# Band by GpSimd on the exponentials, and the NF4 planes summed by TensorE alone, in a fused four-layer kernel

## The chip, the cores and the metric

The kernel runs on one core of one Trainium2 chip. The metric is the device time of one launch in microseconds. Engines are named as in the profile: PE is TensorE (PEld its weight loads), DVE is VectorE, ACT is ScalarE, POOL is GpSimd, SP is SyncE, which only issues transfers.

## The reference

x has 16 batches of 128 rows by 512 columns. Four layers are added to it in turn, each on its layer norm: a first attention, a feed-forward layer with NF4 weights, a cross attention, and a layer of 32 experts. Only two pieces matter here. The first attention sees a batch as 512 tokens of 128 channels (8 heads of 16), and a query attends only to keys at a distance of 64 or less:

```python
scores = jnp.einsum('bqhd,bkhd->bhqk', q, k) / jnp.sqrt(jnp.asarray(d, q.dtype))
band = jnp.abs(idx[:, None] - idx[None, :]) <= local_size        # local_size = 64
scores = jnp.where(band[None, None], scores, neg)
attn = jax.nn.softmax(scores, axis=-1)
o = jnp.einsum('bhqk,bkhd->bqhd', attn, v).reshape(n, t, e)
```

The weights of the feed-forward layer go through NF4 and back: blocks of 64 are divided by their largest magnitude, each value is replaced by the nearest of 16 levels, and the result is multiplied by the (again quantized) block scale.

```python
idx = jnp.argmin(jnp.abs(scaled[:, None] - NF4), axis=-1)
```

## The kernel before

Everything that the change touches is in `phase_layer0_attention`, the first 490 us. Each engine has a program of its own, written out by hand, and they meet only by semaphores; the order on an engine is the order of the code. All of them run `batches`, a body for each of the 16 batches i (the first two and the last two written out, the rest as a hardware loop over pairs). In a batch there are two units u = 2i and 2i + 1, one for each half of the heads, and in a unit eight steps c.

For the attention, a step c has three parts on TensorE: the maxima of the *next* batch (`smax`, L505: two products of 192 or 256 columns in one of two banks `ps_max`), the scores of this one (`scores`), and now and then a piece of other work. In `scores` one bank `ps_sc` (again two, taken in turn) holds one head against two key tiles, transposed: keys on the partitions, the window of 256 queries around each key tile in the columns. The first product into the bank (L520) is identity times `band_mask`, 448 columns, which puts 0 inside the band and -1e30 outside; the two products of L525 add the scores to it. ScalarE turns the bank into exponentials in `probs_t` (`exps`, L383, 448 columns f32). When four steps are done, `pv` (L537) multiplies the probabilities with the values: at c = 5 for the first half of a unit's steps, at c = 1 of the next unit for the second half. VectorE takes the band's row maxima from `ps_max` (`take_max`, L776, which adds the same mask), two instructions a step. A score may start when the exponential two steps before it is done, a maximum when the one two before it is taken.

Between these runs the NF4 round trip of the weights, one chunk of 512 columns a unit, 33 chunks m in all. VectorE scales a chunk (L898), compares it with eight steps (`nf4_compare`, L908: result (value > step) times the level's height, as f16, two comparisons in each of c = 0 to 3), and at c = 4 adds the eight planes pairwise to four (L912, 128x2048 elements). ScalarE makes seven more planes with a sign function (L377). TensorE sums the four and the seven planes in `ps_nf4` during the next unit (`nf4_sum`, L571), as the table `NF_AT` has it for c = 0 to 7, and VectorE multiplies the sum with the block scale (L918). So VectorE's and ScalarE's work in a unit belongs to chunk m and TensorE's to chunk m - 1.

GpSimd builds constants at the start (the mask with `affine_select`, L294 and L297), and issues the transfers of the block scales through DRAM: L308 and L311 (`gather_maxima`), L315 and L319 (`spread_scales`). After about 117 us it is idle to the end of the stage.

## Time and profile before

| | us |
|---|---|
| median of 3 runs | 1466.27 |
| lowest, highest | 1461.33, 1466.6 |
| profiled execution, first to last instruction | 1463.7 |
| median of the runs less that span | 2.6 |

Busy in the whole span: TensorE 93%, VectorE 69%, ScalarE 54%, GpSimd 17%. These shares are means over four very different stages. The change touches the first, so only what stands in 0 to 490 us says what it is worth. An engine's busy time there is that of drawn instructions; matmuls are drawn with a tail that overlaps the next, so pitches, from start to start, tell more of TensorE. The granted TensorE clock was 0.98 of full speed between 100 and 200 us and 1.00 from there to 400, that is 2.4 GHz.

### The profile page before, as it was taken

Reading aid. Unit: us, or ns where it says so; the run is one execution under the profiler, and the core shown is the slowest. Engines: PE = TensorE matmul, PEld = TensorE weight load, DVE = VectorE, ACT = ScalarE, POOL = GpSimd, SP = SyncE. Lnnn points to the kernel's source line nnn. Section 1 sums busy time; section 2 is a strip of 40 time slices with the busy share of each in tenths; the row PEclk is TensorE's granted clock in tenths of the full one; section 3 lists DMA queues with packets and bytes.
Section 4 is the critical chain, followed back from the end, with each engine's and each line's share of the span. In section 5 each row is a group of like instructions: output and inputs, shape, how many; then the busy total and the mean of one; then the engine's idle time right before and its main releaser. Section 6 shows DMA issues by size and latency. Waiting matters only on the chain. (4 is left out here: it accounts for less than half of the span.)

```text
span 1463.7 us, 28639 instructions
## 1 busy us (share of the span) xinstructions
PE 1354.5 (93%) x8666; PEld 813.1 (56%) x8666; DVE 1002.8 (69%) x3234; ACT 791.5 (54%) x1802; POOL 249.2 (17%) x265
## 2 busy tenths in 40 slices
PE   3678999999999799999989999999789999999998
PEld 1345555555555444444455555555434777777774
DVE  8889999999997646456546788887659654545211
ACT  4777888888888733332357677776530233332331
POOL 4100000000000100000010000002411255555552
PEclk7699999999999999999999999999999999999999
DMA  8534344343440300000020000000322588888885
GB/s 261 145 87 99 91 107 106 86 119 90 107 104 17 145 1 0 0 0 0 0 75 15 16 16 14 14 1 2 146 85 93 184 247 251 255 257 246 255 233 115
DMA packets 63186, 149.52 MB, mean 102 GB/s; under 512 B 10792, under 2 KB 27830, under 8 KB 58892
## 3 DMA queue, kind: packets, MB, share of 16 engines
q1 hardware_dynamic: 49836, 115.70, 26.1%
q0 software_dynamic: 13280, 32.93, 9.6%
q8 instruction: 38, 0.62, 0.2%
q14 instruction: 32, 0.26, 0.1%
HBM read 113.21 MB, written 35.39 MB: 102 GB/s over the span
## 5 line engine op out<-in xcount | busy, mean ns | idle before, releaser
L776 DVE CUSTOM_DVE_ANT_0 masked_scores<-ps_max,band_mask 128x192 bf16<-128x192 f32 (+1 forms) x512 | 177.2, 383 | 20.5 <-PE ps_max L505 13.9
L383 ACT ACTIVATE probs_t<-ps_sc 128x448 f32<-128x448 f32 x256 | 138.7, 542 | 80.4 <-PE ps_sc L525 78.1
L1255 PE MATMUL f_ps<-f_xt,w_t 128*128 (+1 forms) x704 | 160.2, 382 | 2.5 <-ACT w_t L1310 2.5
L377 ACT ACTIVATE nf_above<-nf_scaled,nf_sign_at 128x512 f16<-128x512 bf16 x231 | 161.5, 715 | 0.0
L2803 DVE TENSOR_TENSOR d_inter<-d_silu_g,d_su 128x384 f32<-128x384 f32 x32 | 17.7, 554 | 159.6 <-PE d_su L2487 154.4
L1927 ACT ACTIVATE c_probs<-d_sg,c_negmax 128x128 f32<-128x128 f32 x256 | 90.3, 365 | 58.1 <-DVE c_negmax L2012 57.7
L1255 PEld LDWEIGHTS f_ps<-f_xt,w_t 128*128 128x128 bf16 x704 | 69.3, 98 | 86.7 <-issue 5.0
L2320 POOL DMA_INDIRECT out<-d_h,d_scatter_now x64 | 97.2, 1519 | 108.3 <-DMA out<-d_h,d_scatter_now 92.9
L505 PE MATMUL ps_max<-k_stack,q_stack 96*128 96x192 bf16 (+1 forms) x512 | 96.5, 272 | 19.8 <-DVE row_max L776 13.8
L2671 DVE TENSOR_SCALAR d_onehot<-d_slot_no,d_pos 128x192 bf16<-128x192 bf16 x512 | 101.0, 288 | 0.3 <-PE d_lb L2388 0.3
L505 PEld LDWEIGHTS ps_max<-k_stack,q_stack 96*128 96x128 bf16 x512 | 46.2, 101 | 92.1 <-issue 46.9
L520 PE MATMUL ps_sc<-band_mask,identb 128*128 128x448 bf16 x256 | 92.7, 362 | 2.5 <-ACT probs_t L383 2.5
L2481 PE MATMUL d_su<-d_h,d_wgu 128*128 128x192 f32 x512 | 93.7, 337 | 1.4 <-DVE d_h L2790 1.0
L525 PE MATMUL ps_sc<-q_stack,k_stack 98*128 98x192 bf16 (+1 forms) x512 | 93.2, 263 | 0.0
L2481 PEld LDWEIGHTS d_su<-d_h,d_wgu 128*128 128x128 f32 x512 | 84.4, 194 | 9.8 <-issue 9.8
L2487 PE MATMUL d_su<-d_h,d_wgu 128*128 128x192 f32 x512 | 88.4, 326 | 0.0
L1429 DVE SCALAR_TENSOR_TENSOR f_h<-f_ps,f_h_scale,f_silu 128x512 f32<-128x512 f32 x44 | 32.9, 748 | 76.7 <-PE f_ps L1255 76.6
L2487 PEld LDWEIGHTS d_su<-d_h,d_wgu 128*128 128x128 f32 x512 | 84.1, 190 | 0.0
L2012 DVE TENSOR_REDUCE c_negmax<-d_sg 128x4 f32<-128x512 f32 x64 | 44.0, 688 | 50.7 <-PE d_sg L1705 49.9
L571 PE MATMUL ps_nf<-nf_above,nf_half_step 128*128 128x512 f16 x231 | 75.8, 380 | 0.0
L1336 ACT ACTIVATE f_hparts<-f_h 128x512 f16<-128x512 f32 x44 | 27.7, 630 | 86.0 <-DVE f_h L1429 86.0
L525 PEld LDWEIGHTS ps_sc<-q_stack,k_stack 98*128 98x128 bf16 x512 | 51.3, 100 | 28.7 <-issue 3.0
(381 smaller groups left out, 2830.1 us busy)
## 6 DMA issues: line engine op xcount, KB each, us to landing
d_wgu<-in_ex_gu SPq DMA_DIRECT2D x32, 1024.0 KB
d_wdown<-in_ex_d SPq DMA_DIRECT2D x32, 512.0 KB
dr_parts<-qk_parts SPq DMA_DIRECT2D x32, 384.0 KB, 4.8
q_stack<-dr_parts SPq DMA_DIRECT2D x32, 192.0 KB, 2.7
k_stack<-dr_parts SPq DMA_DIRECT2D x32, 192.0 KB, 3.3
out<-x_sb SPq DMA_DIRECT2D x21, 256.0 KB, 2.2
nf_w<-in_nf_w POOLq DMA_DIRECT2D x3, 1408.0 KB, 10.2
q_stack<-dr_parts SPq DMA_DIRECT2D x32, 128.0 KB, 2.4
```

The lines of the kernel that those rows point to most:

```text
L377: act.activation(above[:, g, k, :], lvl[:, g, :], ACT.Sign, bias=cut[:, k - NDV:k - NDV + 1]).then_inc(s_sg, 1)
L383: act.activation(pt[:, c, :], SP[c % 2][:].rearrange("p a w -> p (a w)")[:, a:z], ACT.Exp, scale=D0 ** -0.5).then_inc(s_e, 1)
L505: mm = pe.matmul(m[:, k, off:off + hi - lo], qst[0:96, b, h, qt * P:qt * P + P], kst[0:96, b, h, lo:hi], start=True, stop=True)
L520: pe.matmul(s[:].rearrange("p a w -> p (a w)")[:, a:z], identb[:], mask[:].rearrange("p a w -> p (a w)")[:, a:z], start=True, stop=False)
L525: mm = pe.matmul(s[:, k, off:off + hi - lo], kst[0:98, b, h, kt * P:(kt + 1) * P], qst[0:98, b, h, lo:hi], start=False, stop=(k == 1))
L776: op = dve.tensor_tensor_reduce(masked[:, c % 2, k, off:off + hi - lo], M[c % 2][:, k, off:off + hi - lo], mask[:, k, off:off + hi - lo], ...
L1255: mm = pe.matmul(bank[:], w12[:, m, kt, ft * P:(ft + 1) * P], xt[:, q, kt, bass.ds(g * N, N)], start=(kt == 0 and q == 0), stop=(kt == KT ...
L1927: op = act.activation(pr[:, ot % 2, j, :], SB[ot % 2][:, j, :], ACT.Exp, bias=nm[:, ot % 2, j:j + 1], accum_out=sm[:, bb, 4 * ot + j:4 * o ...
L2320: pool.indirect_dma_start(out, bass.IndirectOffsetOnAxis(ap=sst[rows_of[a], par, a:a + 1], axis=0), yo[a][:, par, :], None, compute_op=ALU ...
L2481: mm = pe.matmul(GP[:, it, :], wg[:, par, t, it * P:(it + 1) * P], xt[:, par, t, :], start=(t == 0), stop=(t == KT - 1))
L2487: mm = pe.matmul(UP[:, it, :], wg[:, par, t, FI + it * P:FI + (it + 1) * P], xt[:, par, t, :], start=(t == 0), stop=(t == KT - 1))
L2671: op = dve.tensor_scalar(oh[:, half, tl, jj, :], ios[:], pos[:, half * HT + tl, bass.ds(4 * q + jj, 1)], None, ALU.is_equal)
```

## The change

It has two parts.

1. *The band.* The mask product L520 goes; the scores' two products each start their own region of the bank. ScalarE's exponential is then of unmasked scores, and GpSimd sets the elements outside the band to zero afterwards, by two `affine_select` a step, each over 2 x 128 columns of `probs_t`, in place (`band`). `pv` waits for the select's semaphore `s_in` and no longer for the exponential's. `probs_t` gets full windows (8 x 2 x 256), whose outer 64 columns are set to zero once and aren't written by the exponentials. GpSimd's transfers of the block scales now stand between its selects. The maxima still use the mask on VectorE.
2. *The planes.* The add L912 goes; TensorE sums all eight comparison planes and the seven sign planes, 15 matmuls a chunk in place of 11.

```diff
@@ gpsimd @@
+            def band(u, c):
+                pool.wait_ge(s_e, 8 * u + c + 1)
+                pool.nop(nofuse=True)
+                low, high = pt[:, c, :, 0:P], pt[:, c, :, P:WIN]
+                pool.affine_select(out=low, in_=low, compare_op=ALU.is_ge, fill=0.0, base=0,
+                                   pattern=[[0, 2], [1, P]], channel_multiplier=-1)
+                pool.affine_select(out=high, in_=high, compare_op=ALU.is_ge, fill=0.0, base=0,
+                                   pattern=[[0, 2], [-1, P]], channel_multiplier=1).then_inc(s_in, 1)
+            def body(j, i, b, first, last, final):
+                for c in range(8):
+                    band(2 * i, c)
+                if first:
+                    pool.wait_ge(s_sc, 1)
+                    spread_scales(0, 1)
+                for c in range(8):
+                    band(2 * i + 1, c)
+                    if c == 4 and isinstance(i, int) and i == 1:
+                        pool.wait_ge(s_sc, 2)
+                        spread_scales(1, 3)
+                if first:
+                    pool.wait_ge(s_am, 5)
+                    gather_maxima(1, 3)
@@ scores @@
-                pe.matmul(s[:].rearrange("p a w -> p (a w)")[:, a:z], identb[:],
-                          mask[:].rearrange("p a w -> p (a w)")[:, a:z], start=True, stop=False)
...
-                                   qst[0:98, b, h, lo:hi], start=False, stop=(k == 1))
+                                   qst[0:98, b, h, lo:hi], start=True, stop=True)
@@ pv @@
-                pe.wait_ge(s_e, 8 * u + 4 * kp + 4)
+                pe.wait_ge(s_in, 8 * u + 4 * kp + 4)
@@ NF4 @@
-            NF_AT = [[], [0, 2], [4, 6], [8], [9, 10], [11], [12, 13], [14]]
+            NF_AT = [[], [0, 1], [2, 3], [4, 5], [6, 7, 8], [9, 10], [11, 12], [13, 14]]
...
-                if c == 4:
-                    dve.wait_ge(s_ab, NF_INC * m + 4)
-                    dve.tensor_tensor(above[:, g, 0:8:2, :], above[:, g, 0:8:2, :], above[:, g, 1:8:2, :], ALU.add).then_inc(s_ab, 1)
```

How this moves instructions is seen at two places. The first is TensorE in the loop, steps c = 1 and 2 of a unit, before:

```order
L520 MATMUL ps_sc<-band_mask,identb 128x448 [waits a_exp]
L525 MATMUL ps_sc<-q_stack,k_stack 128x192
L525 MATMUL ps_sc<-q_stack,k_stack 128x256
L530 ISA
L537 MATMUL ps_o<-probs_t,v_ones 32x256 [waits a_exp]
L537 MATMUL ps_o<-probs_t,v_ones 32x256 x3
L537 MATMUL ps_o<-probs_t,v_ones 32x192 x4
L565 ISA
L571 MATMUL ps_nf<-nf_above,ident_f 128x512 [waits a_nf4_done,a_nf4_above]
L571 MATMUL ps_nf<-nf_above,ident_f 128x512
```

and now, for the same steps of an earlier unit (the line numbers are those of the changed kernel):

```order
L549 MATMUL ps_sc<-q_stack,k_stack 128x192 [waits a_exp]
L549 MATMUL ps_sc<-q_stack,k_stack 128x256
L561 MATMUL ps_o<-probs_t,v_ones 32x256 [waits a_probs_in_band]
L561 MATMUL ps_o<-probs_t,v_ones 32x256 x3
L561 MATMUL ps_o<-probs_t,v_ones 32x192 x4
L595 MATMUL ps_nf<-nf_above,ident_f 128x512 [waits a_nf4_done,a_nf4_above]
L595 MATMUL ps_nf<-nf_above,ident_f 128x512
```

The mask product is gone and the probability product waits for another semaphore; at c = 4 three planes are summed where there were two, and the order of everything else is kept. The second place is GpSimd around its first transfer of block scales (`dr_rep<-sc_bf`), before:

```order
L303 DMA nf_w<-in_nf_w 128x4x1408
L315 DMA dr_rep<-sc_bf 88x128 [waits a_sc]
L319 DMA block_scale<-dr_rep 128x11x8 [waits a_rep_wr]
L308 DMA dr_sc<-absmax 128x11x8 [waits a_block_max]
L308 DMA dr_sc<-absmax 128x4x22
```

and now:

```order
L344 AFFINE_SELECT probs_t<-probs_t 128x2x128 [waits a_exp]
L346 AFFINE_SELECT probs_t<-probs_t 128x2x128
L316 DMA dr_rep<-sc_bf 88x128 [waits a_sc]
L320 DMA block_scale<-dr_rep 128x11x8 [waits a_rep_wr]
L344 AFFINE_SELECT probs_t<-probs_t 128x2x128 [waits a_exp]
L346 AFFINE_SELECT probs_t<-probs_t 128x2x128
```

Eight pairs of selects now stand ahead of the transfer, and the ninth waits behind it and behind what it waits for.

## Rows read from the trace of the kernel before

**Rows 1.** The windows view, two stretches; "(x...)" counts instructions.

```profile
core 0: us, PE busy (x) PEld busy (x) DVE busy (x) ACT busy (x) POOL busy (x), PEclk, DMA share, GB/s
459.00:478.00 19.00, 18.45 (x151) 9.84 (x149) 11.35 (x30) 17.81 (x35) 0.00 (x0) 1.00 0.05 16
200.00:226.14 26.14, 24.96 (x197) 14.59 (x197) 24.80 (x100) 21.61 (x40) 0.00 (x0) 1.00 0.41 101
```

**Rows 2.** Line L810 (add to x): its register step, once a batch.

```profile
L810 DVEq FUSED_REGOPS  x12: 65/65/65, 144.8 to 432.3; - x12
```

**Rows 3.** Waits, 200 to 400 us: total, times, longest us.

```profile
PEld ps_max L505 <- DVE row_max L776: 5.3, 19, 0.4
...
DVE masked_scores L776 <- PE ps_max L505: 4.1, 8, 0.7
```

**Rows 4.** Groups, 200 to 400 us: busy us, mean ns, idle before.

```profile
L571 PE MATMUL ps_nf<-nf_above,nf_half_step 128*128 128x512 f16 x106 | 35.3, 379 | 0.0
L908 DVE TENSOR_SCALAR nf_above<-nf_scaled 128x512 f16<-128x512 bf16 x124 | 29.9, 281 | 0.0
...
L912 DVE TENSOR_TENSOR nf_above<-nf_above 128x2048 f16<-128x2048 f16 x15 | 18.2, 1210 | 0.0
```

**Rows 5.** Timeline, TensorE at 306 and 480: start us, duration us, instructions.

```profile
305.94 0.35 PE L520 MATMUL ps_sc<-band_mask,identb 128*128 128x448 bf16 x1
...
306.13 0.25 PE L525 MATMUL ps_sc<-q_stack,k_stack 98*128 98x192 bf16 x1
...
480.25 1.03 PE L571 MATMUL ps_nf<-nf_above,ident_f 128*128 128x512 f16 x4
```

**Rows 6.** Timeline, GpSimd's selects at the start.

```profile
1.87 0.28 POOL L292 TENSOR_SCALAR_AFFINE_SELECT ident<-ident 128x128 f32<-128x128 f32 x1 [0.24 <-POOL band_mask L289]
2.12 0.28 POOL L292 TENSOR_SCALAR_AFFINE_SELECT identb<-identb 128x128 bf16<-128x128 bf16 x1
2.37 0.61 POOL L294 TENSOR_SCALAR_AFFINE_SELECT band_mask<-band_mask 128x512 bf16<-128x512 bf16 x1
```

**Rows 7.** Timeline, 8.5 to 17 us: GpSimd's memset and VectorE's conversions.

```profile
8.61 6.92 POOL L327 MEMSET k_stack<- 2x8192 bf16 x1
...
10.37 5.24 DVE L818 CAST ident_f<-ident 128x128 f16<-128x128 f32 x1
...
15.75 0.21 DVE L820 TENSOR_SCALAR nf_half_step<-ident 128x128 f16<-128x128 f32 x1
```

**Rows 8.** Views of L2671 (1183.5 to 1187.6 us) and L2057: min/median/max ns.

```profile
L2671 DVE TENSOR_SCALAR d_onehot<-d_slot_no,d_pos x16: 249/257/570, 1183.7 to 1187.2; 128x192 bf16<-128x192 bf16 x16
...
L2057 DVE TENSOR_TENSOR x_sb<-x_sb,c_out x16: 677/680/692, 812.9 to 1052.7; 128x512 f32<-128x512 f32 x8, 128x512 f32 x8
```

**Rows 9.** Timeline, GpSimd in three later stretches.

```profile
1015.23 17.08 POOL L1608 TENSOR_SCALAR c_next_rows<-x_sb,c_next_mv,c_next_rstd 128x512 f32<-128x512 f32 x8 [24.03 <-DVE c_next_rstd L2113]
...
1106.52 0.50 POOL L2283 COPY d_quad_vals<-d_slot_vals 128x384 bf16<-128x384 bf16 x1 [23.38 <-DVE d_tmp L2761]
...
1183.92 1.09 POOL L2283 COPY d_quad_vals<-d_slot_vals 128x384 bf16 x1
```

**Rows 10.** Timeline, 314 to 318 us: exponential and probability product.

```profile
314.77 0.54 ACT L383 ACTIVATE probs_t<-ps_sc 128x448 f32<-128x448 f32 x1 [0.45 <-PE ps_sc L525]
...
316.98 0.96 PE L537 MATMUL ps_o<-probs_t,v_ones 128*32 128x256 f32 x16
```

**Rows 11.** Timeline, 478 to 486 us: the stage's end.

```profile
478.01 0.59 PEld L537 LDWEIGHTS ps_o<-probs_t,v_ones 128*32 128x32 f32 x16 [0.76 <-ACT probs_t L383]
...
482.81 1.23 DVE L912 TENSOR_TENSOR nf_above<-nf_above 128x2048 f16<-128x2048 f16 x1
...
485.22 1.02 PE L571 MATMUL ps_nf<-nf_above,ident_f 128*128 128x512 f16 x4 [0.18 <-ACT nf_above L377]
```

**Rows 12.** Timeline, GpSimd's transfers of the block scales.

```profile
90.69 0.79 POOL L311 DMA_DIRECT2D sc_blocks<-dr_sc  x1 [4.34 <-DMA dr_sc<-absmax]
...
114.97 1.91 POOL L319 DMA_DIRECT2D block_scale<-dr_rep  x2 [1.65 <-DMA dr_rep<-sc_bf]
```

More of the change, by code:

```diff
@@ L109, in phase_layer0_attention @@
     mparts = sb("max_parts", [16, 2, P], BF16)
-    pt = sb("probs_t", [P, 8, 2 * WIN - BAND], F32)
+    pt = sb("probs_t", [P, 8, 2, WIN], F32)
     oc = sb("o_cols", [P, D], F32)
@@ L174, in phase_layer0_attention @@
     s_s, s_e, s_pv = sem("a_scores"), sem("a_exp"), sem("a_pv")
+    s_in, s_pad = sem("a_probs_in_band"), sem("a_probs_pad")
     s_oc, s_oT, s_rs, s_on = sem("a_o_copy"), sem("a_o_turn"), sem("a_o_recip"), sem("a_o_norm")
@@ L204, in phase_layer0_attention @@
     PRODUCTS = [(qst, 0, [(0, 0, 2), (2, 0, 3), (5, 0, 1)]), (kst, 1, [(0, 0, 3), (3, 0, 1), (4, 0, 2)])]
-    NF_INC = 5
+    NF_INC = 4
     MEAN_AT = D - 4
@@ L336, in _ @@
             load_nf(2)
-            pool.wait_ge(s_sc, 1)
-            spread_scales(0, 1)
-            pool.wait_ge(s_am, 5)
-            gather_maxima(1, 3)
-            pool.wait_ge(s_sc, 2)
-            spread_scales(1, 3)
+            def band(u, c):
[20 more added lines that the diff above has]
+                    gather_maxima(1, 3)
+            pool.wait_ge(s_ko, 1)
+            pool.memset(pt[:, 0:4, 0, 0:BAND], 0.0).then_inc(s_pad, 1)
+            pool.wait_ge(s_pad, 1)
+            pool.memset(pt[:, 4:8, 1, WIN - BAND:WIN], 0.0).then_inc(s_pad, 1)
+            pool.wait_ge(s_pad, 2)
+            batches(pool, body)
         @block.scalar
@@ L382, in exps @@
                 a, z = kept(c // 4)
-                act.activation(pt[:, c, :], SP[c % 2][:].rearrange("p a w -> p (a w)")[:, a:z], ACT.Exp, scale=D0 ** -0.5).then_inc(s_e, 1)
+                act.activation(pt[:, c].rearrange("p a w -> p (a w)")[:, a:z], SP[c % 2][:].rearrange("p a w -> p (a w)")[:, a:z], ACT.Exp, scale=D0 ** -0.5).then_inc(s_e, 1)
             def o_copy(u, g):
@@ L518, in scores @@
                 s = SP[c % 2]
-                a, z = kept(kp)
-                pe.matmul(s[:].rearrange("p a w -> p (a w)")[:, a:z], identb[:],
-                          mask[:].rearrange("p a w -> p (a w)")[:, a:z], start=True, stop=False)
                 for k in range(2):
@@ L537, in pv @@
                         mm = pe.matmul(O[32 * j:32 * j + 32, lo:hi], va[:, b, kt, 4 * g + j, :],
-                                       pt[:, 4 * kp + j, k * WIN + off - kept(kp)[0]:k * WIN + off - kept(kp)[0] + hi - lo],
+                                       pt[:, 4 * kp + j, k, off:off + hi - lo],
                                        start=(kt == 0), stop=(kt == QT - 1), skip_group_check=True)
@@ L573, in nf4_sum @@
                     mm.then_inc(s_lm, 1)
-            NF_KS = [0, 2, 4, 6] + list(range(8, NLV))
-            NF_AT = [[], [0, 2], [4, 6], [8], [9, 10], [11], [12, 13], [14]]
+            NF_KS = list(range(NLV))
+            NF_AT = [[], [0, 1], [2, 3], [4, 5], [6, 7, 8], [9, 10], [11, 12], [13, 14]]
             def nf4_mean(lo, hi):
```

## The prediction, made before the changed kernel was run

> **What bounds the kernel now.** I read the windows first, since the change touches one stage only, the first attention (0 to 490 us of the span); then the groups of instructions in its steady part, the waits there, and last the timeline, where pitches and gaps can be seen. One batch takes (432.3 - 144.8) / 11 = 26.14 us: the line that adds to x runs once a batch, and its register step ran twelve times between those two starts [rows 2]. In a stretch of exactly one batch VectorE is busy 24.80 us, TensorE 24.96 us (with modelled ends), ScalarE 21.61 us and GpSimd 0 [rows 1]. The reader is to see three engines near full and one empty. Which of the first two is the bound is decided by the waits: VectorE waited on TensorE for only 4.1 us in 200 us, and TensorE's loads on VectorE's maxima for 5.3 us, on the same two banks [rows 3]. The stretch 459 to 478, the last batch, settles it. There are no maxima of a next batch there, VectorE is busy 11.35 of 19.00 us, and the same 16 exponentials take 19 us in place of 26 [rows 1]. That batch also lacks 32 maximum products and the projections on TensorE, so it doesn't prove VectorE alone, but it is then ScalarE that is full (17.81 of 19.00). I take VectorE as the bound of the steady batch, with TensorE close behind: TensorE's matmuls are shown with a tail (a 448-column product is drawn at 0.35 us, but the next starts 0.19 us later), so its true load is less than it looks [rows 5].
>
> **Part one: the sum of the planes.** It removes one VectorE add of 128x2048 f16 per chunk, 33 in all, 1.21 us each [rows 4]: two per batch, 2.42 us of VectorE's 24.80. It adds four matmuls of 512 columns per chunk on TensorE. Four such matmuls in a row take 1.03 us [rows 5], and one alone is drawn at 0.38 [rows 4]: (1.03 - 0.38) / 3 = 0.217 us each, so 8 x 0.217 = 1.7 us per batch. They are laid out two or three behind each score; the order shows none on its own wait.
>
> **Part two: the band.** It removes the mask product of each score from TensorE, 16 a batch at a pitch of 0.19 us [rows 5], 3.0 us. TensorE so ends 3.0 - 1.7 = 1.3 us a batch lighter, and stays behind VectorE. ScalarE's work is unchanged. GpSimd gets two selects of 128x256 f32 behind each exponential, 32 a batch. The trace has selects of 128 columns (start to start 0.25 us, drawn at 0.28) and of 512 (0.61) [rows 6]: (0.61 - 0.28) / 384 = 0.86 ns a column, so 256 columns have a pitch near 0.36 us, and 32 of them are 11.5 us of a batch. GpSimd is thus at work some 45% of the time, and keeps up.
>
> **The wait for the band.** The probability products now wait for the select instead of the exponential. From the end of an exponential to both selects is about 0.1 + 0.36 + 0.39 = 0.85 us. The last exponential that a second-half product needs ended at 314.77 + 0.54 = 315.31, and the product began at 316.98: 1.7 us of slack [rows 10]. The first-half product stands behind the score two places after its last exponential, as this one does, and is no nearer. So the selects hide, as long as they aren't held up by more than 0.8 us. Behind a product that waited stand all of TensorE's later maxima and scores. I count 0 in the steady batches.
>
> **What GpSimd costs VectorE.** This is the term that decides, and it isn't in the diff. At the start a VectorE cast of 128 columns is drawn at 5.24 us, and it ends just when GpSimd's 6.92 us memset does; the same size takes 0.21 us once GpSimd is idle [rows 7]. Later, GpSimd's copy of 384 columns (L2283) takes 0.50 us at 1106.5, and 1.09 us at 1183.9 beside VectorE's tensor_scalars on bf16 (L2671); in that stretch one of the tensor_scalars takes 570 in place of 249 ns [rows 8, 9]. So a VectorE operation of this kind and a GpSimd operation exclude each other, and one meeting costs VectorE about 570 - 249 = 0.32 us. The 16 comparisons a batch (L908, 281 ns, in pairs) are of that kind [rows 4]. Not all VectorE work is: the add of two SBUF tensors at L2057 took 677 to 692 ns in all 16 places, which come about every 16 us, so that one at least fell into the 17 us in which GpSimd ran without a gap [rows 8, 9]; and reads of PSUM, the maxima above all, weren't seen held. Bounds per batch: below, 0 meetings, 0 us; above, every comparison meets a select, 16 x 0.32 = 5.1 us. I take 5 meetings: GpSimd works 45% of the time, so about 4 of 8 pairs find a select under way, and now and then one slips in between the two of a pair. 5 x 0.32 = 1.6 us.
>
> A rule of the Trainium skill speaks against this change more strongly (SBUF — State Buffer, Who interferes with whom): GpSimd has only the port pair that VectorE uses as its second, and "a DVE instruction with two SBUF inputs contends with a GpSimd instruction that reads SBUF". By that the three kinds with two SBUF inputs would be held too, which is the third rival below; without the rule the sum stays as it is. The trace agrees on the exclusion for the comparisons' kind and shows no such delay at L2057.
>
> **The sum**, against the profiled execution: span 1463.7 us, with 2.6 us around it up to the median of 1466.27.
> - Batches 0 to 14: 15 x (-2.42 + 1.6) = -12.3 us.
> - Last batch: 0. ScalarE is the bound there, and its work is the same [rows 1].
> - The tail (478 to 490): here TensorE is followed in order. Eight more matmuls at 0.217 are +1.7; the last probability product had waited for its exponential, so the selects' 0.9 us is fully seen. The add at 482.81 to 484.04 was over before the sum that needed it began at 485.22, so its removal gives nothing [rows 11]. +2.6 us.
> - The start: GpSimd's DMAs of the block scales now stand between selects. Its wait of 4.34 us for a DMA (before L311) holds the selects of the third group, whose product comes 8 scores later; three more issues and a wait near 1.7 us stand inside the fourth group [rows 12]. I take +1.0, between 0 and about 6.
> - Sum: -8.7 us. 1466.3 - 8.7 = 1457.6 us.
>
> **What is late next.** Without the add VectorE has 22.4 us, with the meetings 24.0; TensorE some 23.7 as drawn; ScalarE 21.6. All three lie within 10%, so each loses something to the others' order; the 1.34 us that VectorE now idles per batch is kept as it is.
>
> **The rivals.**
> - *Hardly a meeting.* GpSimd's selects fall mostly beside the maxima. One or no meeting a batch: 15 x (-2.42 + 0.3) + 3.6 = -28; with none -32.7. 1434 to 1438 us. For it: selects follow exponentials, comparisons follow maxima, and their phases may stay apart. Against: the rows of the gather stage, where meetings came in each group.
> - *Slower: the selects and comparisons meet nearly every time.* The place is VectorE at L908; the price 0.32 us a meeting; it decides from 2.42 / 0.32 = 7.6 meetings a batch on. When VectorE is delayed, it frees TensorE's bank later, scores come later and bunch, and the selects bunch with them. With 11 of 16: 15 x (3.5 - 2.42) + 3.6 = +20: 1486 us; with all 16, +44: 1510.
> - *Two-input operations are held as well.* Third parts (2), scaled weights (2) and the gate (1) are five more a batch, at half chance and 0.32: 0.8 us. 15 x (-2.42 + 1.6 + 0.8) + 3.6: about 1470 us.
> - *The wait for the band takes the removed work's place.* If GpSimd is held by comparison pairs (0.48 us) and one slow operation, the 0.8 us of spare at the second-half product is used up. Four products a batch at 0.5 us are 2.0, against the 1.3 that TensorE gains: 15 x 0.7 + 3.6, about 1480 us if TensorE is then the bound. Against it: the 1.7 us of slack [rows 10].
>
> **How the numbers follow.** The smallest change a measurement of this kernel can tell is about 0.5%, 7.3 us: faster is below 1459, slower above 1473.6. The forecast case (3 to 7 meetings, 1448 to 1467) has 0.40, of which 0.24 falls below 1459 and 0.16 within. Hardly a meeting: 0.24, faster. Two-input: 0.12, of it 0.08 within and 0.04 slower. Band wait: 0.08, 0.02 within and 0.06 slower. Meetings nearly always: 0.16, slower. Together: faster 0.48, the same 0.26, slower 0.26. The range reaches from no meeting (1434) to 11 or 12 of 16 (1488); the forecast case's own is 1448 to 1467.
>
> **What would show it.** The group of the 128x2048 add is gone and VectorE's share in a batch falls below 24 us. The comparisons' median stays near 281 ns, but their maximum rises to 600 ns or so, and their mean to 281 + 1600 / 16, near 380 ns; at 281 the first rival holds, over 430 the second. Third parts (L751), scaled weights (L898) and the gate (L757) keep the lengths that they have before, or the third rival holds. Selects are drawn near 0.39 us, some at 0.6 to 0.9. In the waits, the probability products show GpSimd as releaser only in the last batch and the tail. The register step of the add to x comes every 25.3 us. The forecast is wrong if that period lies above 26.1, or if TensorE or ScalarE shows idle time ended by GpSimd in the steady batches.

## The result, and the profile after

The changed kernel takes 1469.54 us (median of 20 runs, 1467.01 to 1473.52), the kernel before 1466.02 us (20 runs): a ratio of 1.0031, interval 1.0021 to 1.0040. By the prediction's bound of 0.5% this is no change. It is slower all the same, by 3.5 us in the medians and by 3 to 6 us by the interval, where 8.7 us less were forecast. Its profiled execution took 1467.35 us, with a span of 1465.6 us.

In the changed file the lines have moved: L908 is now L932 (comparisons), L898 L922, L751 L775, L757 L781, L776 L800 (maxima), L571 L595 (planes), L537 L561 (probability product), L810 L834 (add to x), L383 L410 (exponential). The selects are L344 and L346.

The windows, of one batch and of a stretch inside the last one, answer to [rows 1]; line L834's register step to [rows 2].

```profile
core 0: us, PE busy (x) PEld busy (x) DVE busy (x) ACT busy (x) POOL busy (x), PEclk, DMA share, GB/s
200.00:225.76 25.76, 23.68 (x190) 13.81 (x189) 23.63 (x102) 21.87 (x40) 15.19 (x33) 1.00 0.40 103
456.00:475.00 19.00, 17.02 (x141) 9.19 (x141) 9.65 (x28) 17.41 (x34) 12.13 (x31) 1.00 0.06 17
```

```profile
L834 DVEq FUSED_REGOPS  x12: 65/65/65, 143.2 to 426.6; - x12
```

The period is (426.6 - 143.2) / 11 = 25.76 us, 0.38 less than before. VectorE and TensorE both lost over 1 us of work a batch, and both now stand idle for some 2 us. The waits from 200 to 400 us (total, times, longest) say on whom:

```profile
POOL probs_t L344 <- ACT probs_t L410: 83.7, 102, 1.9
...
DVE masked_scores L800 <- PE ps_max L532: 13.2, 22, 1.0
PEld ps_max L532 <- DVE row_max L800: 11.7, 35, 0.5
...
PE ps_g L538 <- DVE o_rows L827: 6.7, 8, 0.8
PE ps_g L538 <- DVE x_sb L834: 5.2, 7, 0.8
```

In [rows 3] the first two waits between VectorE and TensorE were 4.1 and 5.3 us; the last two, TensorE's transposes of the maxima waiting at the turn of a unit, had these rows in the kernel before:

```profile
PE ps_g L511 <- DVE o_rows L803: 5.1, 8, 0.6
...
PE ps_g L511 <- DVE x_sb L810: 3.9, 7, 0.6
```

So each engine waits longer for the other than before. The probability product waits for GpSimd in no row of this stretch. The groups there (busy us, mean ns, idle before), and the views of four lines of VectorE (min/median/max ns), answer to [rows 4, 8]:

```profile
L344 POOL TENSOR_SCALAR_AFFINE_SELECT probs_t<-probs_t 128x256 f32<-128x256 f32 x125 | 64.6, 517 | 83.7 <-ACT probs_t L410 83.7
L346 POOL TENSOR_SCALAR_AFFINE_SELECT probs_t<-probs_t 128x256 f32<-128x256 f32 x125 | 60.4, 483 | 0.0
L932 DVE TENSOR_SCALAR nf_above<-nf_scaled 128x512 f16<-128x512 bf16 x124 | 35.1, 323 | 0.0
L922 DVE SCALAR_TENSOR_TENSOR nf_scaled<-nf_w,absmax_recip 128x512 bf16 x16 | 12.5, 779 | 0.0
```

```profile
L932 DVE TENSOR_SCALAR nf_above<-nf_scaled x264: 270/286/865, 45.0 to 480.2; 128x512 f16<-128x512 bf16 x132
L922 DVE SCALAR_TENSOR_TENSOR nf_scaled<-nf_w,absmax_recip x33: 672/693/975, 43.5 to 466.8; 128x512 bf16 x24, 128x512 bf16<-128x512 bf16 x9
L775 DVE TENSOR_TENSOR qk_parts<-qk_resid,qk_parts x32: 683/692/877, 18.0 to 414.1; 128x512 bf16<-128x512 f32 x32
L781 DVE TENSOR_TENSOR gated<-relu_o,ctx_tile x16: 686/686/847, 112.4 to 484.4; 128x512 f32<-128x512 f32 x16
```

Meetings are there and are cheap: the comparisons' mean is 323 ns against 281 before, 16 x 0.042 = 0.67 us a batch, and the two scaled weights cost 2 x (0.779 - 0.678) = 0.20 more. The timeline of VectorE shows the single meetings. These are the held comparisons and the two scaled weights of one batch; a comparison that isn't held takes about 0.28 us (0.47 to 0.49 a pair), a scaled weight 0.67:

```profile
225.85 0.50 DVE L932 TENSOR_SCALAR nf_above<-nf_scaled 128x512 f16<-128x512 bf16 x1
226.27 0.89 DVE L922 SCALAR_TENSOR_TENSOR nf_scaled<-nf_w,absmax_recip 128x512 bf16 x1
228.29 0.69 DVE L932 TENSOR_SCALAR nf_above<-nf_scaled 128x512 f16<-128x512 bf16 x2
...
239.50 0.67 DVE L922 SCALAR_TENSOR_TENSOR nf_scaled<-nf_w,absmax_recip 128x512 bf16 x1
240.66 0.70 DVE L932 TENSOR_SCALAR nf_above<-nf_scaled 128x512 f16<-128x512 bf16 x2
```

The pairs left out (at 236.19, 237.28 and 239.10, and from 248.21 to the end of the batch at 251.6) aren't held. So three comparisons and one scaled weight are held a batch, each by some 0.21 us. GpSimd pays most of it: an undisturbed select is drawn at 0.41 us, the mean is 0.50, and 32 x 0.09 = 2.9 us a batch.

Just behind the rolled loop (the hardware loop over batches 2 to 13) is something the forecast did not have. The timeline of TensorE (start, duration, instructions, idle before):

```profile
427.57 0.27 PE L538 MATMUL ps_g<-ident,row_max 128*16 128x128 f32 x1 [0.66 <-issue]
427.68 0.38 PE L532 MATMUL ps_max<-k_stack,q_stack 96*128 96x256 bf16 x2
427.89 0.35 PE L549 MATMUL ps_sc<-q_stack,k_stack 98*128 98x192 bf16 x2
428.18 0.95 PE L561 MATMUL ps_o<-probs_t,v_ones 128*32 128x256 f32 x12
431.68 0.52 PE L561 MATMUL ps_o<-probs_t,v_ones 128*32 128x192 f32 x4 [2.55 <-issue]
```

TensorE stands 2.55 us between the twelfth and the thirteenth of the sixteen drawn matmuls of one probability product (the profile draws each of its eight twice). It waits for no engine ("issue"); TensorE has no such gap there in the kernel before. The tail's timeline answers to [rows 11]:

```profile
475.72 0.96 PE L561 MATMUL ps_o<-probs_t,v_ones 128*32 128x256 f32 x16 [0.70 <-POOL probs_t L346]
...
483.79 1.89 PE L595 MATMUL ps_nf<-nf_above,ident_f 128*128 128x512 f16 x8 [0.18 <-ACT nf_above L404]
485.51 1.67 PE L595 MATMUL ps_nf<-nf_above,nf_half_step 128*128 128x512 f16 x7
```

Here the product does wait for the select, and eight matmuls stand where four stood.

### The profile page after: what moved, and what is told of

It reads as the page before. It is cut to its first block and busy times, and to the rows that moved or that the text cites. A ratio compares the mean times of both kernels' runs of the same rounds, so it can differ in the third digit from the quotient of the medians.

```text
span 1465.6 us, 29315 instructions
## 1 busy us (share of the span) xinstructions
PE 1336.3 (91%) x8542; PEld 800.7 (55%) x8542; DVE 980.7 (67%) x3201; ACT 794.8 (54%) x1802; POOL 488.0 (33%) x779
## 5 line engine op out<-in xcount | busy, mean ns | idle before, releaser
L800 DVE CUSTOM_DVE_ANT_0 masked_scores<-ps_max,band_mask 128x192 bf16<-128x192 f32 (+1 forms) x512 | 176.6, 384 | 32.8 <-PE ps_max L532 29.6
L344 POOL TENSOR_SCALAR_AFFINE_SELECT probs_t<-probs_t 128x256 f32<-128x256 f32 x256 | 128.2, 501 | 173.7 <-ACT probs_t L410 173.4
L410 ACT ACTIVATE probs_t<-ps_sc 128x448 f32<-128x448 f32 x256 | 139.1, 544 | 71.3 <-PE ps_sc L549 65.8
L346 POOL TENSOR_SCALAR_AFFINE_SELECT probs_t<-probs_t 128x256 f32<-128x256 f32 x256 | 123.6, 483 | 2.0 <-ACT probs_t L410 2.0
L1623 POOL TENSOR_TENSOR x_sb<-x_sb,c_bp 128x512 f32 x16 | 21.1, 1319 | 210.1 <-DVE c_xq L1995 210.0
L1615 POOL MEMSET c_k_diag<- 128x4096 f32 x1 | 3.5, 3512 | 248.0 <-DVE c_xq L1995 248.0
L595 PE MATMUL ps_nf<-nf_above,ident_f 128*128 128x512 f16 x264 | 79.9, 388 | 2.9 <-DVE nf_w L939 2.7
```

The source lines that it names most:

```text
L344: pool.affine_select(out=low, in_=low, compare_op=ALU.is_ge, fill=0.0, base=0, pattern=[[0, 2], [1, P]], channel_multiplier=-1)
L346: pool.affine_select(out=high, in_=high, compare_op=ALU.is_ge, fill=0.0, base=0, pattern=[[0, 2], [-1, P]], channel_multiplier=1).then_inc ...
L410: act.activation(pt[:, c].rearrange("p a w -> p (a w)")[:, a:z], SP[c % 2][:].rearrange("p a w -> p (a w)")[:, a:z], ACT.Exp, scale=D0 ** ...
L800: op = dve.tensor_tensor_reduce(masked[:, c % 2, k, off:off + hi - lo], M[c % 2][:, k, off:off + hi - lo], mask[:, k, off:off + hi - lo], ...
```

## The experiments

The table gives every run by its ratio to the kernel before of the same job and by five numbers of its one profile: the period of the rolled batches (register steps over 11), the first batch behind the loop, the time from the last add to x but one to the last (the tail, with the last batch's end), TensorE's own stall behind the loop, and for how long in that batch the granted clock was 0.50, that is 1.2 GHz.

| run | median us | ratio (interval) | period | behind the loop | tail | stall | low clock |
|---|---|---|---|---|---|---|---|
| before | 1466.02 | | 26.14 | 26.57 | 10.53 | none | 3.4 |
| changed | 1469.54 | 1.0031 (1.0021-1.0040) | 25.76 | 28.91 | 13.03 | 2.55 | 3.4 |
| e1_planes_only | 1477.26 | 1.0088 (1.0071-1.0104) | 26.85 | 25.73 | 12.26 | none | none |
| e2_band_only | 1479.17 | 1.0105 (1.0086-1.0124) | 26.75 | 26.16 | 11.63 | none | 3.4 |
| e3_no_band | 1462.34 | 0.9990 (0.9978-1.0002) | 25.34 | 28.17 | 12.28 | 2.26 | 3.4 |
| e4_spare_tile | 1469.11 | 1.0028 (1.0014-1.0042) | 25.75 | 28.91 | 12.30 | 2.54 | 3.4 |
| e5_no_add | 1459.41 | 0.9966 (0.9953-0.9979) | 25.82 | 24.36 | 10.53 | none | none |
| e6_no_mask | 1460.65 | 0.9983 (0.9970-0.9996) | 25.57 | 25.32 | 11.19 | none | 3.4 |
| e7_add_at_end | 1468.26 | 1.0029 (1.0017-1.0041) | 25.75 | 29.20 | 11.29 | 2.85 | 3.4 |
| e8_changed_again | 1469.10 | 1.0034 (1.0021-1.0047) | 25.75 | 29.47 | 13.01 | 3.13 | 3.4 |
| e9_turn_later | 1468.36 | 1.0023 (1.0008-1.0037) | 25.51 | 30.43 | 13.03 | 3.27 | 6.8 |
| e10_before_turn_later | 1458.46 | 0.9951 (0.9935-0.9967) | 25.67 | 24.83 | 10.53 | none | none |
| e11_32_nops | 1469.76 | 1.0043 (1.0027-1.0059) | 25.75 | 30.54 | 13.03 | 2.82 | 6.8 |
| e12_before_both_turns | 1456.11 | 0.9951 (0.9934-0.9968) | 25.45 | 24.58 | 10.53 | none | none |
| e13_changed_both_turns | 1462.25 | 0.9985 (0.9972-0.9998) | 25.27 | 25.45 | 13.11 | 1.58 | none |
| e14_16_nops | 1470.66 | 1.0044 (1.0029-1.0060) | 25.75 | 28.68 | 13.02 | 2.32 | 3.4 |
| e15_8_nops | 1469.24 | 1.0030 (1.0017-1.0043) | 25.75 | 29.21 | 13.02 | 2.86 | 3.4 |
| e16_nops_inside | 1469.12 | 1.0028 (1.0010-1.0046) | 25.76 | 30.17 | 13.02 | 2.97 | 6.8 |
| e17_nops_behind | 1470.86 (one) | | 25.76 | 30.37 | 13.01 | 2.40 | 6.8 |
| e18_four_halved | 1466.03 | 1.0014 (1.0003-1.0025) | 25.76 | 24.39 | 13.03 | none | none |

### Each part alone

e1 is the kernel before with the planes summed unfolded and the mask product kept:

```
-    NF_INC = 5
+    NF_INC = 4
-    NF_KS = [0, 2, 4, 6] + list(range(8, NLV))
+    NF_KS = list(range(NLV))
     (NF_AT as in the changed kernel)
-    if c == 4: dve.wait_ge(...); dve.tensor_tensor(above[:, g, 0:8:2, :], ..., ALU.add)
```

> The kernel before with the second part of the change alone: VectorE's pairwise add of planes is gone, TensorE sums 15 planes a chunk, the mask product stays and GpSimd has no selects. Theory A (VectorE stays the bound of a steady batch, and GpSimd's selects take the gain away): period 26.14 - 2.42 + something under 0.5, about 24.0 to 24.3 us in place of 26.14, the whole 25 to 32 us faster than before. Theory B (TensorE becomes the bound as soon as VectorE is lighter, whoever does the band): TensorE gains 1.7 us of work a batch, the period stays at 25.8 us or above, the whole within 6 us of before.

e2 is the changed kernel with the add kept and 11 plane products, the reverse of those lines.

> The kernel before with the first part of the change alone: no mask product, the band set to zero by GpSimd behind each exponential, VectorE's add of planes kept. Theory A (selects cost VectorE, which is the bound): VectorE gets about 0.9 us more a batch and saves nothing, so the period is 26.6 to 27.2 us and the whole 8 to 20 us slower than before. Theory B (TensorE the bound): TensorE is 3.0 us a batch lighter, so the whole is faster by up to 10 us.

Each part alone makes the kernel slower, by 0.9 and 1.05%. For e2 that is what the first theory had; e1 came out slower than either of its theories. One batch of e1 in the windows view (columns as above), then one of e2:

```profile
200.00:226.85 26.85, 25.98 (x204) 15.57 (x204) 22.90 (x99) 21.55 (x40) 0.00 (x0) 1.00 0.38 98
```

```profile
200.00:226.75 26.75, 22.36 (x184) 12.83 (x180) 25.80 (x102) 21.59 (x40) 14.60 (x33) 1.00 0.39 98
```

In e1 the full engine is TensorE: it has 1.7 us more, and the period is 0.71 us longer although VectorE lost 2.42. In e2 it is VectorE, 25.80 of 26.75 us, and the meetings lengthen what is full. So the parts can't be added up: each part takes from one engine and gives to the other, and the two together undo each other's harm.

### The selects: port or wait?

e3 has no selects (the band isn't applied), e4 runs them on a spare tile, and the product waits for the exponential alone:

```
 e3  -  band(2 * i, c) ... batches(pool, body)
     -  pe.wait_ge(s_in, 8 * u + 4 * kp + 4)
     +  pe.wait_ge(s_e, 8 * u + 4 * kp + 4)
 e4  +  ge(pool, s_in, 8 * u + c)             # each pair of selects behind the one before
     -  low, high = pt[:, c, :, 0:P], pt[:, c, :, P:WIN]
     +  low, high = spare[:, :, 0:P], spare[:, :, P:WIN]
     and the same wait as e3
```

> The changed kernel with the band left out: neither mask product nor selects, probability products wait for the exponentials; GpSimd issues its transfers as before the change. Theory A (selects are what eats the gain): period near 23.8 to 24.2 us against 25.76 in the changed kernel, the whole 25 to 35 us faster than before. Theory B (the selects are cheap, the rest of the chain between TensorE, ScalarE and VectorE is the limit): period 25 us or more, the whole under 15 us faster. Theory C (the later stages are slower whatever the first stage does): the stages behind 490 us take some 2 to 3 us longer than in the kernel before here too.

> The changed kernel, but GpSimd's selects, in number, shape and time of release the same, work on a spare tile, and the probability products wait for the exponentials; the band is left out of the result. Only what GpSimd does to VectorE is left, not the wait for it. If the meetings on VectorE are the cost, it is as the changed kernel in the steady batches: 25.6 to 25.8 us a batch. If the wait for the band is the cost, it is as the one without selects, near 24 us. In the last two batches and the tail the wait for the selects is gone in any case, 2 to 4 us of the 5 us that the changed kernel loses there.

With the selects and no wait on them the period is 25.75 us, as changed; without the selects it is 25.34. So the wait for the band costs nothing in a steady batch, and GpSimd's work beside VectorE costs 0.41 us. VectorE's busy time in one batch grows by more, 0.69 us (23.63 against 22.94 in e3), or 0.87 by the means of the two groups above. e3's group of comparisons is back at 281 ns:

```profile
L912 DVE TENSOR_SCALAR nf_above<-nf_scaled 128x512 f16<-128x512 bf16 x124 | 29.9, 281 | 0.0
```

In the tail the wait is seen: 13.03 against 12.28 and 12.30 us. With the last batch, 0.6 us shorter in e4, that is 1.3 us, where the expectation of e4 had 2 to 4.

### One relief at a time

e5 is the kernel before without the add (TensorE still sums 11 planes, so the four odd planes of each chunk aren't in the sum), e6 without the mask product (no band on the scores):

```
 e5  -  dve.tensor_tensor(above[:, g, 0:8:2, :], ..., ALU.add)
 e6  -  pe.matmul(s[...][:, a:z], identb[:], mask[...][:, a:z], start=True, stop=False)
```

> The kernel before with VectorE's pairwise add taken out and nothing put in its place: TensorE still sums 11 planes a chunk, so four comparison planes are left out of the weights. VectorE is 2.42 us a batch lighter, TensorE is unchanged. Theory V (the prediction's: VectorE bounds the steady batch): period 26.14 - 2.42 and a little, 23.8 to 24.5 us, the whole 25 to 35 us faster. Theory T (TensorE and its waits at the turn of a unit bound it): period 25.8 to 26.1 us, the whole faster by 0 to 5 us.

> The kernel before with the mask product taken out and nothing put in its place: the band is left out of the result. TensorE is 3.0 us a batch lighter, VectorE, ScalarE and GpSimd are unchanged. Theory V (VectorE is the bound): period 26.0 us or more, the whole within 3 us of before. Theory T (TensorE is the bound, half of what it is relieved of comes through until VectorE is full): period 24.9 to 25.8 us, the whole 6 to 18 us faster.

2.42 us less for VectorE bring 0.32 us a batch, 3.0 us less for TensorE 0.57, both together (e3, with 1.7 us given back to TensorE) 0.80. The waits of e5, 200 to 400 us:

```profile
DVE masked_scores L776 <- PE ps_max L505: 16.0, 24, 1.0
...
PEld ps_max L505 <- DVE row_max L776: 11.9, 35, 0.4
```

VectorE waited 4.1 us for the maxima's products before [rows 3] and now 16.0: of the 2.42 us removed, (16.0 - 4.1) / 7.7 batches = 1.5 us come back as waiting. TensorE's loads, too, wait more for VectorE (11.9 us against 5.3), though VectorE has less to do. Neither engine as a whole is the bound, then. What else could be, the points at which the two hand over to each other, is tested under "The turns". The period of e6 is as expected by its second theory, but the whole fell by less than the 6 us it had as its least.

### The tail, and the changed kernel again

e7 is the changed kernel with the add and 11 products kept for the last two chunks, e8 the changed kernel unedited.

```
+  if c == 4 and isinstance(m, int) and m >= NCH - 2:
+      dve.tensor_tensor(above[:, g, 0:8:2, :], ..., ALU.add).then_inc(s_ab, 1)
```

> The changed kernel with VectorE's pairwise add kept for the last two chunks only, where the steady batches are over and VectorE idles; TensorE then sums 11 planes for these two and 15 for the others. If the eight further matmuls stand on the path at the stage's end, as the prediction's tail term has it, the stretch from the second last to the last add to x is 1.6 to 1.8 us shorter than in the changed kernel (13.0 us there), and the whole 1.5 to 2 us faster than it, that is 0 to 3 us slower than before. If that stretch hangs on something else, it stays at 13 us.

> The changed kernel once more, for a second profile and more times on the chip that the others share. Ratio to before 1.002 to 1.004. If the stages behind 490 us, which took 977.5 us in its first profile against 975.1 us in that of the kernel before, are longer for a reason in the kernel, they take 977 us or more again; if that was the spread between executions, the second profile lies anywhere between 974 and 979.

The tail gives back 1.7 us, the eight matmuls as priced. The whole hardly shows it (1.0029 against 1.0034): the stall and the start differ as much from one execution to the next.

### The turns

TensorE's transposes of a unit's maxima (max_t) stand in front of the next unit's scores and wait there for VectorE. e10 moves the one of the second half one step later in the kernel before, and VectorE's step that reads it behind that step's comparisons; e9 does so in the changed one. e12 and e13 also put a probability product ahead of each such transpose.

```
 e9, e10    -  if c == 0: (wait) max_t(2 * i + 1, 1)
            +  if c == 1: (wait) max_t(2 * i + 1, 1)
               and max_parts(2 * i + 1, 1) on VectorE behind the comparisons of step 1,
               no longer ahead of them
 e12, e13   +  pv(2 * i - 1, 1 - b, 1, 1) before that wait
            +  pv(2 * i, b, 0, 1) before the waits of max_t(2 * i + 2, 0)
```

> The changed kernel with one handshake moved: at the turn to a new batch TensorE turns the row maxima (the transposition at L538 into ps_g) one step later, behind the scores of step 1 and no longer behind those of step 0, and VectorE reads them behind its comparisons of step 1. All work is the same. In the changed kernel TensorE stands 1.7 us a batch before these transpositions, waiting for VectorE's last work of the unit before (o_rows, the add to x). Theory T (the batch is bound by the two engines waiting for each other in order, at the turn of a unit, and not by either one's work): moving one of the two takes 0.3 to 0.8 us out of a batch, period 25.0 to 25.5 us, the whole 5 to 12 us faster than the changed kernel. Theory W (work bounds it): period 25.7 us as before.

> The kernel before with the same handshake moved by one step. TensorE stands 1.5 us a batch before the transpositions there. Theory T: period 25.6 to 25.9 us in place of 26.14, the whole 3 to 9 us faster than before. Theory W: 26.1 us.

> The kernel before with the transposes that VectorE waits for issued one step later, as in the run before, and now both handshakes of a batch behind a probability product: TensorE has that product to do while VectorE ends what it needs. Theory A (what bounds the batch is that two nearly full engines meet at the turn of each unit): VectorE's waits for TensorE and TensorE's for VectorE shrink, period 25.0 to 25.5 us against 25.67, whole 1452 to 1457 us. Theory B (the work of either engine bounds it and the meeting is only where it shows): period 25.6 to 25.8, whole 1457 to 1460. If VectorE in its turn gets its operand too late, the period is above 26 and the whole above 1462.

> The changed kernel with the same two moves as the run beside it. Theory A (the meeting of the engines bounds the batch): the relief of VectorE comes through, period 25.0 to 25.4 us against 25.76 as changed and 25.51 with one move, whole 1460 to 1466 us. Theory B (TensorE's own work, 22.2 us and more of each batch, bounds it by now): period 25.5 to 25.8, whole 1467 to 1470. By both the stall after the loop's end and the longer tail (13 us after the last batch but one) stay.

No engine does less work, and the period of the kernel before falls by 0.47 us with one move and 0.69 with both, more than the whole change under study brings (0.38). Of the two waits at the turn, 5.1 and 3.9 us, the second is gone from the waits of e10 and both from those of e12. That of the changed kernel falls by 0.25 and 0.49. The whole of e9 gained far less than the 5 to 12 us expected; its batch behind the loop is the second longest of the table. In e12 VectorE has hardly a gap left, one batch of it:

```profile
200.00:225.45 25.45, 24.83 (x198) 14.51 (x197) 24.89 (x102) 21.38 (x39) 0.00 (x0) 1.00 0.41 104
```

VectorE's idle time is 0.56 us there, where it was 1.34 [rows 1]. In e13 a new wait appears, the product that now comes earlier waits for the selects:

```profile
PEld ps_o L561 <- POOL probs_t L346: 7.2, 8, 0.9
```

e10 and e12 beat both kernels (0.9951 each); between these two the time can't be told apart, though the period can.

### The stall behind the loop

e11, e14, e15 put 32, 16 and 8 empty instructions on TensorE ahead of the loop, e17 16 behind it, e16 one ahead of each score.

```
+  for k in range(32):            # 16 in e14, 8 in e15
+      pe.nop(nofuse=True)
   batches(pe, body)
```

> The changed kernel with 32 empty TensorE instructions ahead of the rolled loop, which do no work and only move where TensorE's later instructions lie in its code. Theory A (the 2.3 to 3.3 us in which TensorE stands in the middle of a probability product just after the loop hang on where its code lies): the stall leaves that place or shrinks, the time between the last batch's predecessor and it (28.9 and 29.5 us in two profiles of the changed kernel) falls to 25.5 to 27, and the whole to 1465.5 to 1467.5 us, 0.999 to 1.001 of the kernel before. Theory B (it does not hang on the place): the stall stays at 2.3 to 3.3 us, the batch at 28.5 to 29.5, the whole at 1468 to 1470 (1.0015 to 1.0035). The period of the rolled batches is 25.75 us by both.

> The changed kernel with 16 empty TensorE instructions ahead of the rolled loop, half as many as the run with 32, which left the 2.3 to 3.3 us stall of TensorE at the same instruction (after the twelfth matmul of the first probability product behind the loop). Theory A (32 was a whole number of the pieces in which code arrives, so that run moved nothing): here the stall moves to another instruction or goes, and with it some 2 us of the batch after the loop (28.9 to 30.3 us in the changed kernel; 26 to 27 without it) and of the whole, 1466 to 1468 us. Theory B (the place of the code doesn't matter): the stall stays after the twelfth matmul, 2.3 to 3.3 us, the whole 1468.5 to 1470.5.

> The changed kernel with 8 empty TensorE instructions ahead of the rolled loop. Theory A: the stall moves to an instruction between those of the run with none and the run with 16, or goes. Theory B: it stays after the twelfth matmul of that product, 2.3 to 3.3 us, the whole 1468.5 to 1470.5 us.

> The changed kernel with one empty TensorE instruction ahead of each score, 16 a batch, 32 in the rolled loop's body of two batches. By my count of two instructions a matmul (weights and product) the kernel before has 32 x (1 mask product) less 16 x (1 plane sum) more in it than the changed one, 32 a body, so that the loop now ends as far from its start as there. Theory C (the stall behind the loop hangs on how long the loop's body is, as profiles of bodies 32 longer, 32 shorter and 48 longer show none): it is gone, the batch behind the loop takes 26 to 27.5 us, the whole 1466 to 1468.5 us if the empty instructions cost the steady batch nothing (period 25.75). Theory D (it does not, but on what the changed kernel's TensorE does): the stall stays at 2.3 to 3.3 us and the whole at 1468.5 to 1471.

> The changed kernel with 16 empty TensorE instructions just behind the rolled loop, run once. Theory C (a fixed number of instructions from the loop's start): the stall comes some 8 matmuls earlier in the work, after about the fourth of the product's sixteen matmuls, and is as long or longer. Theory D: it stays after the twelfth.

The stall stayed at the same matmul in e11, e14, e15 and e17. This is no evidence: the built program keeps one of the empty instructions ahead of the loop and none of the 16 behind it, so these four are in effect the changed kernel again (and give its spread: stall 2.32 to 3.13 us in its six profiles, batch behind the loop 28.7 to 30.5). e16 keeps four in the loop's body of two batches, not the 32 it was meant to add, so it doesn't test its theories either; there the stall came two drawn matmuls earlier, as long as before:

```profile
439.31 0.86 PE L561 MATMUL ps_o<-probs_t,v_ones 128*32 128x192 f32 x6 [2.97 <-issue]
```

The length of TensorE's rolled body, counted in the built programs, then sorted all runs: 396 (e2, e6), 428 (before, e5, e10, e12) and 444 (e1) without the stall, 412 (changed and its kin, e3, e4, e7, e9, e13) and 416 (e16) with it. e18 tests this with real instructions: four planes of each chunk in two halves, 428 in the body.

```
+  if k in (1, 2, 3, 4):
+      for lo in (0, 256):
+          mm = pe.matmul(NF[:, lo:lo + 256], ident16[:], above[:, g, k, lo:lo + 256], ...)
```

> The changed kernel with four of the fifteen planes of each chunk summed in two halves of 256 columns, which is the same work in 8 more matmuls a batch. TensorE's rolled body of two batches so has 428 instructions in the built program, as that of the kernel before, where the changed one has 412. (The runs with empty instructions shifted nothing: the build keeps 1 of the 32, 16 or 8 ahead of the loop, 4 of the 32 inside it and none of the 16 behind it.) Bodies of 396, 428 and 444 showed no stall of TensorE behind the loop, bodies of 412 and 416 all did, 2.3 to 3.3 us. Theory C (the stall hangs on the length of the body): it is gone, and from the last but three to the last but two add to x, the batch behind the loop, 26 to 27.5 us pass in place of 28.9 to 30.3; the whole 1466 to 1468.5 us. Theory D (it hangs on what else the kernels with 412 share, all with the mask product and the add gone): the stall stays at 2.3 to 3.3 us and the batch at 28.5 to 30.5; the whole 1468.5 to 1471.

TensorE's timeline at the same place in e18:

```profile
430.59 0.35 PE L549 MATMUL ps_sc<-q_stack,k_stack 98*128 98x192 bf16 x2
430.87 0.96 PE L561 MATMUL ps_o<-probs_t,v_ones 128*32 128x256 f32 x16
431.77 0.39 PE L599 MATMUL ps_nf<-nf_above,ident_f 128*128 128x512 f16 x1
432.00 0.38 PE L597 MATMUL ps_nf<-nf_above,ident_f 128*128 128x256 f16 x2
432.21 0.38 PE L532 MATMUL ps_max<-k_stack,q_stack 96*128 96x256 bf16 x2
```

Sixteen matmuls without a gap; the batch takes 24.39 us in place of 28.7 to 30.5, the period is unchanged at 25.76, and the ratio falls from 1.0031 to 1.0014, some 2.5 us. So TensorE's stall came with the 16 instructions that the change took out of the body, and it goes when 16 others are put in. In every run, e18 too, such an edit moved the code ahead of the loop and behind it as well, so whether the length counts or the place isn't told apart.

TensorE's stall is not all that happens in this batch. VectorE, too, stands for no engine there, 1.15 to 1.86 us in all 20 profiles. In the kernels that keep VectorE's add throughout (before, e2, e6, e10, e12) it does so where TensorE waits for it, 1.7 to 2.2 us. In the kernel before:

```profile
442.54 0.42 DVE L776 CUSTOM_DVE_ANT_0 masked_scores<-ps_max,band_mask 128x256 bf16<-128x256 f32 x1 [1.86 <-issue]
443.97 0.65 PE L545 MATMUL ps_g<-ident,o_cols 128*128 128x128 f32 x4 [1.84 <-DVE v_ones L762]
```

In or behind such a gap of TensorE the granted clock fell to 0.50 in most profiles (the windows view, columns as above; the kernel before, then the changed one):

```profile
446.00:448.00 2.00, 2.00 (x15) 0.96 (x16) 2.00 (x9) 2.00 (x5) 0.00 (x0) 0.50 0.04 8
```

```profile
434.00:436.00 2.00, 2.00 (x11) 1.29 (x10) 2.00 (x8) 0.76 (x2) 1.45 (x4) 0.50 0.03 9
```

It stayed there for 3.4 or 6.8 us (last column of the table). With gaps of 1.58 to 1.86 us it fell in the kernel before and not in e10, e12 and e13; in e4 it fell only behind a later gap of 1.06 us; with none above 1.1 us (e1, e5, e18) it didn't fall. An estimate of the price is half the time at half the clock, 1.7 or 3.4 us. It fits: 24.39 of e18, the changed kernel's stall of 2.55 and 1.7 are 28.6, against 28.91 measured; with e11's 2.82 and 3.4 they are 30.6, against 30.54; and e10's 24.83, with the same gap of VectorE and the full clock, and 1.7 are 26.5, against the 26.57 of the kernel before.

## Why the prediction was wrong

By stretch, the changed kernel's six profiles (its own, e8, and in effect e11, e14, e15, e17) against the one of before: up to the first register step +1.0 us (145.8 mean, 143.2 to 146.9, against 144.8), eleven rolled batches -4.2, the batch behind the loop +3.0 (29.5), the last one +0.4, the tail +2.5, all that follows +1.1 (976.2 mean, 975.4 to 977.5, against 975.1). Sum +3.8 us; the medians differ by 3.5. The forecast was -8.7, so 12.5 us are to be explained: 4.8 in the rolled batches, 2.5 in the stretch before them, 3.8 in the batch behind the loop, and 1.4 in what is left.

The sign of being wrong that it named, a period above 26.1 us, did not come: 25.76 lies between that and the 25.3 forecast. That the third rival's total, 1470 us, is what was measured is chance: its own term was 0.2 us a batch, not 0.8, and 3.8 us of the miss lie in the batch behind the loop, which no rival had.

- **What bounds the kernel: the step that failed.** "I take VectorE as the bound of the steady batch, with TensorE close behind". The sum let all of VectorE's balance through, and none of TensorE's. The runs show that of 2.42 us taken from VectorE alone 0.32 come through, of 3.0 us taken from TensorE alone 0.57, and that moving two handovers without any less work brings 0.69. In its place the handovers between the two bound the batch (e10, e12). The rows for it stood in the waits of the kernel before, 5.1 and 3.9 us at the turns of the units; the text read the two directions of one wait (4.1 and 5.3 us on `ps_max`), took them as small, and did not look at these. The last batch, said to settle it, had no turn with a next batch either, and so couldn't. This is 4.8 us of the miss in the rolled part (eleven batches at -0.38 in place of -0.82). Three batches before it were booked as gains of 2.5 us in all; that stretch was forecast at -1.5 us with the start's +1.0 and came out at +1.0.
- **The cost of meetings.** Forecast 1.6 us of VectorE a batch, all on the comparisons, as 5 meetings of 0.32; measured 0.7 to 0.9 of VectorE, of which 0.41 shows in the period. Both factors were too high: three comparisons are held a batch, and each by 0.21 us. GpSimd bears most of the waiting, 2.9 us. Had the bound been right, this would have made the forecast too slow.
- **Two-input operations.** The third rival was right in kind: L922 rose to 779 ns in the mean, L775 and L781 reached 877 and 847 ns at most, with medians within 10 ns of before. Its price was 0.2 us a batch, not 0.8: one scaled weight held by 0.21. This supports the Trainium skill (SBUF — State Buffer, Who interferes with whom), which has VectorE operations with two SBUF inputs contend with a GpSimd instruction that reads SBUF; the 677 to 692 ns of L2057 [rows 8] had been read as speaking against it, and no run here explains them.
- **The wait for the band.** Right: nothing in steady batches (e4), 0.7 us in the tail. The 1.7 us of slack [rows 10] held, until e13 moved the product forward.
- **The tail and the start.** The tail was right: +2.5 for +2.6, and +1.7 of it is the eight matmuls (e7). The start's term can't be told: its stretch spreads by 3.7 us.
- **The batch behind the loop.** No step had it: -0.8 forecast, +3.0 found, and 2.5 us of the whole are gone in e18, which has a batch of 24.39. The change took 16 instructions out of TensorE's rolled body (32 mask products gone, 16 plane products added); with 16 put back the stall is gone. Without it the change is still not a gain (1.0014). The kernel before had paid a part of this already, 1.7 us by the estimate for its 3.4 us at 1.2 GHz, which is most of why the difference isn't the 5.1 us between 29.5 and 24.39.
- **Not settled.** Why the programs with bodies of 412 and 416 stall and the others don't. The Trainium skill (Runtime: NRT & Kernel Launch, Instruction fetch mechanics) says that an engine streams its code in blocks of 256 instructions and that crossing one is mostly hidden. No run shows the size of such a block, and by the page crossing one would have cost little. The stall does sit at a place in the code: with four more instructions in the body (e16) it comes two drawn matmuls earlier, and where a transpose stands behind the product and no longer ahead of it (e13) two later. Nor is it shown why the clock fell behind some gaps and not behind others. The +1.1 us after the stage lies in the spread of kernels of either kind (974.7 to 978.4) and isn't put down to the change.

## What to carry to other kernels

Where two engines are each about 95% busy and work in written orders, neither need be the bound by itself: look at the points at which one hands over to the other, price a relief of one engine at a small part of its size (here 0.13 to 0.19) until a run shows more, and try first to give the waiting engine something else to do there. Work moved to an idle engine that holds up a busy one, and is held by it, can cost less than the number of chance meetings suggests; here the idle one did most of the waiting. After any edit of a rolled loop's body look at the first batch behind the loop: an engine can stand there for no engine, and the granted clock can be low behind such a gap.

## What the runs showed of the hardware

- Behind a hardware loop TensorE stood 1.6 to 3.3 us in the midst of a run of ready matmuls, or not at all; it went with the length of the loop's body (412 and 416 against 396, 428 and 444 instructions). VectorE stood 1.15 to 1.86 us there in all 20 profiles.
- In or behind such gaps the granted clock was 0.50 (1.2 GHz) for 3.4 us in ten profiles and for 6.8 us in four, after it had been 1.00 for all rolled batches.
- A select of 128x256 f32 on GpSimd has a pitch of 0.36 us and is drawn at 0.40 to 0.41; beside VectorE single ones were drawn at up to 1.48 us.
- In steady batches, comparisons on VectorE that met one took about 0.49 us against 0.28, scaled weights 0.89 against 0.67; the longest of the stage were 865 and 975 ns.
- Two matmuls of 256 columns of f16 cost TensorE what one of 512 costs: in e18 the two that begin at 432.00 us are followed by the next product at 432.21, and the one of 512 at 431.77 by them after 0.23.
- From one execution of the same kernel to the next, the stretch before the second add to x differed by 3.7 us (143.2 to 146.9), that after the stage by 2.1; the rolled part between them by 0.1.
